# Denominators of a decayed linear attention: sums over weighted keys, or a scan of key states

## The reference, cut to what matters

```python
q = elu(x @ Wq) + 1 ; k = elu(x @ Wk) + 1 ; v = x @ Wv       # per head
a = sigmoid(x @ Wa + ba + 2)                                 # one decay per token and head
def step(carry, inp):
    S, z = carry
    qt, kt, vt, at = inp
    S = at * S + kt[:, None] * vt[None, :]
    z = at * z + kt
    num = einsum('k,kv->v', qt, S)
    den = einsum('k,k->', qt, z) + 1e-6
    return (S, z), num / den
out = scan(step) ; x1 = layernorm(x + out @ Wo)
```

## Time and profile before

| what | value |
|---|---|
| median of three runs | 1390.17 us |
| profiled execution, its own time | 1394.7 us |
| its span | 1392.8 us |
| linear attention stage | about 0 to 686 us of the span |
| PE busy in the steady part (360 to 420 us) | 59.19 of 60 us |
| DVE, ACT, POOL busy there | 36.08, 47.96, 26.02 of 60 us |
| granted clock of TensorE there | 1.00 |

### The profile page before, as it was taken

How to read it: one execution, slowest core, us unless ns; L and a number is a source line. 1 busy time by engine, 2 the same in 40 slices (tenths; PEclk the granted TensorE clock), 3 DMA queues, 4 the chain that set the end, 5 groups by cost and what they waited for, 6 DMA issues and landing times. The chain is left out here.

```text
span 1392.8 us, 29331 instructions
## 1 busy us (share of the span) xinstructions
PE 1255.3 (90%) x10053; PEld 1079.5 (78%) x10053; DVE 868.1 (62%) x1579; ACT 937.6 (67%) x2118; POOL 715.1 (51%) x645
## 2 busy tenths in 40 slices
PE   5999999999999999999899999944999999997870
PEld 4788888888888888887677777724788888887870
DVE  4456565665656565565468888845566666665664
ACT  3778777787777778787557777735465556655553
POOL 1244433444443344444467777701477777776653
PEclk9999999999999999999999999965899999999895
DMA  5232222322222232222134434323466666666638
GB/s 175 90 103 85 93 84 65 90 69 85 77 93 77 64 90 68 87 69 84 56 99 111 106 94 115 89 55 110 129 159 159 159 159 159 158 153 148 175 54 249
DMA packets 155787, 151.27 MB, mean 109 GB/s; under 512 B 48882, under 2 KB 124250, under 8 KB 155674
## 3 DMA queue, kind: packets, MB, share of 16 engines
q1 hardware_dynamic: 140698, 129.18, 30.3%
q0 software_dynamic: 14976, 20.62, 8.3%
HBM read 113.45 MB, written 33.84 MB: 106 GB/s over the span
## 5 line engine op out<-in xcount | busy, mean ns | idle before, releaser
L568 DVE SCALAR_TENSOR_TENSOR a_qk<-a_qk_exp,a_qk_relu 128x512 f32<-128x512 f32 x124 | 148.8, 1200 | 179.8 <-ACT a_qk_relu L416 179.8
L1889 POOL DMA_INDIRECT sum_rows<-e_y_out,e_target x78 | 128.0, 1642 | 81.9 <-ACT e_y_out L1943 58.3
L367 POOL TENSOR_TENSOR a_key_sum<-a_probs_old,a_probs_new 128x512 f32<-128x512 f32 x64 | 83.3, 1301 | 153.2 <-DVE a_probs_new L578 153.2
L360 POOL TENSOR_SCALAR_AFFINE_SELECT a_decay_old<-a_decay_old 128x512 f32<-128x512 f32 x64 | 40.6, 635 | 232.2 <-ACT a_decay_new L442 232.2
L676 PE MATMUL a_ps_qk<-a_xT_hi,a_w_hi 128*128 128x256 f32 x496 | 146.8, 296 | 6.8 <-ACT a_qk_relu L416 6.3
L676 PE MATMUL a_ps_qk<-a_xT_lo,a_w_hi 128*128 128x256 f32 x496 | 139.4, 281 | 0.0
L676 PE MATMUL a_ps_qk<-a_xT_hi,a_w_lo 128*128 128x256 f32 x496 | 139.3, 281 | 0.0
L440 ACT ACTIVATE a_decay_old<-a_c_rows,a_c_col 128x256 f32<-128x256 f32 x256 | 127.4, 498 | 17.6 <-DVE a_c_col L560 11.5
L415 ACT ACTIVATE a_qk_exp<-a_ps_qk 128x512 f32<-128x512 f32 x124 | 73.4, 592 | 95.8 <-PE a_ps_qk L676 95.3
L1870 POOL DMA_INDIRECT e_x_in<-x_rows,e_index x78 | 80.4, 1030 | 78.2 <-DVE e_index L2036 55.7
L576 DVE TENSOR_TENSOR a_probs_old<-a_ps_old,a_decay_old 128x512 f32<-128x512 f32 x128 | 82.3, 684 | 55.8 <-PE a_ps_o L768 44.3
(11 more groups left out here) (310 smaller groups left out, 4170.8 us busy)
## 6 DMA issues: line engine op xcount, KB each, us to landing
a_c_rows<-a_c_scratch SPq DMA_DIRECT2D x128, 256.0 KB, 3.4
e_gu_raw<-in_L_ffn_gate_w SPq DMA_DIRECT2D x23, 512.0 KB
e_gu_raw<-in_L_ffn_up_w SPq DMA_DIRECT2D x23, 512.0 KB
e_dn_raw<-in_L_ffn_down_w SPq DMA_DIRECT2D x23, 512.0 KB, 5.3
a_x_in<-in_x SPq DMA_DIRECT2D x16, 256.0 KB
a_resid<-in_x SPq DMA_DIRECT2D x16, 256.0 KB, 4.8
x_rows<-a_x SPq DMA_DIRECT2D x16, 256.0 KB, 3.4
x_bo_rows<-a_x_bo SPq DMA_DIRECT2D x16, 256.0 KB, 3.9
```

Source lines behind the costliest of these rows:

```text
L367: pool.tensor_tensor(key_sum[:], probs_old[:, :, P:N], probs_new[:], ALU.add).then_inc(keys_summed, 1)
L568: vec.scalar_tensor_tensor(qk[g][:], qk_exp[buffer][:], 1.0, qk_relu[buffer][:], ALU.min, ALU.add).then_inc(qk_done, 1)
L1889: pool.indirect_dma_start(sum_dram, bass.IndirectOffsetOnAxis(target[par][:, blk:blk + 1], 0), y_out[par][:, blk, :], None, compute_op=ALU ...
```

## The change

Denominators no longer come from the weighted scores. A scan on VectorE builds z for all 256 tokens: for a pair, `tensor_tensor_scan` of 128 features (two heads of 64) x 256 tokens with the decay a, spread over the features' partitions, and the keys. The states are multiplied by the queries on VectorE, split on GpSimd into fp32r parts (a cast and a subtraction), and summed over a head's 64 features by PE with a 128x128 tile that has two blocks of ones. `sum_states(b, k)` stands ahead of `weigh(b, k)` on VectorE, `split_sums` takes the place of `sum_keys` on GpSimd, and PE's `add_keys` of a batch is issued at the batch's end, behind the projections. ScalarE makes a once a sequence, and SyncE stores it and spreads it with four DMAs a batch, each to 64 partitions (L335 of the new kernel). The waits on `o_made` that guarded the weighted scores now are on `weighed`.

```diff
+            def spread_a(b, k):
+                m = b * BATCHES + k
...
+                if m >= 2:
+                    sp.wait_ge(states_done, 2 * (m - 1))
+                for h in range(2):
+                    for p in range(2):
+                        head = 4 * k + 2 * p + h
+                        sp.dma_start(a_rows[m % 2][h * DH:(h + 1) * DH, p, :],
+                                     a_dram[b, head:head + 1, :].to_broadcast([DH, N])).then_inc(a_loaded[m % 2], 16)
...
-            def sum_keys(b, k):
-
-                pool.wait_ge(probs_done, 3 * (b * BATCHES + k + 1))
+            def split_sums(b, g):
+                n = b * PAIRS + g
+                pool.wait_ge(q_states_done, n + 1)
+                if n >= 2:
+                    pool.wait_ge(o_made, n - 1)
                 pool.sem_inc(pool_turns, 1)
-                pool.tensor_tensor(key_sum[:], probs_old[:, :, P:N], probs_new[:], ALU.add).then_inc(keys_summed, 1)
+                pool.tensor_copy(sum_hi[g % 2][:], states[g % 2][:]).then_inc(sum_hi_done, 1)
+                pool.wait_ge(sum_hi_done, n + 1)
+                pool.tensor_tensor(sum_lo[g % 2][:], states[g % 2][:], sum_hi[g % 2][:].bitcast(F32), ALU.subtract)\
+                    .then_inc(sums_split, 1)
...
+            def sum_states(b, k):
+                m = b * BATCHES + k
+                vec.wait_ge(a_loaded[m % 2], 64 * (m // 2 + 1))
+                vec.wait_ge(qk_done, 2 * m + 2)
+                for p in range(2):
+                    if m:
+                        vec.wait_ge(sums_split, 2 * m - 1 + p)
+                    vec.tensor_tensor_scan(states[p][:], a_rows[m % 2][:, p, :], qk[2 * k + p][:, 1, :], 0.0,
+                                           ALU.mult, ALU.add).then_inc(states_done, 1)
+                for p in range(2):
+                    vec.wait_ge(states_done, 2 * m + 1 + p)
+                    vec.tensor_tensor(states[p][:], states[p][:], qk[2 * k + p][:, 0, :], ALU.mult).then_inc(q_states_done, 1)
 
             def weigh(b, k):
                 m = b * BATCHES + k
                 vec.wait_ge(s_made, 2 * m + 2)
-                vec.wait_ge(o_made, 2 * m)
+                vec.wait_ge(weighed, 2 * m)
...
                 for k in range(BATCHES):
+                    sum_states(b, k)
                     weigh(b, k)
...
-                for h in range(2):
-                    pe.matmul(out[h][:, 1, 0:P], ones[:], probs_old[:, 2 * h + p, 0:P], start=True, stop=True)
-                pe.wait_ge(keys_summed, m + 1)
-                for h in range(2):
-                    mm = pe.matmul(out[h][:, 1, P:N], ones[:], key_sum[:, 2 * h + p, :], start=True, stop=True)
-                mm.then_inc(o_made, 1)
...
+            def add_keys(b, g):
+                pe.wait_ge(sums_split, b * PAIRS + g + 1)
+                if b * PAIRS + g >= 2:
+                    pe.wait_ge(oT_done, b * PAIRS + g - 1)
+                pe.matmul(ps_o[g % 2][:, 1, :], head_ones[:], sum_hi[g % 2][:], start=True, stop=False,
+                          skip_group_check=True)
+                pe.matmul(ps_o[g % 2][:, 1, :], head_ones[:], sum_lo[g % 2][:], start=False, stop=True,
+                          skip_group_check=True).then_inc(o_made, 1)
...
                         if k in (1, 2):
                             project_v(b + 1, k - 1, 1)
+                    for p in range(2):
+                        add_keys(b, 2 * k + p)
```

More of the change, by code:

```diff
@@ L167, in sem @@
             return sh.semaphore(nc, name)
-        w_raw = [sb(f"a_w_raw{n}", [P, KC, PW]) for n in range(2)]
+        with nc.sbuf_tensor("a_w_raw0", [P, KC, PW], F32) as first_raw:
+            pass
+        states = [sb(f"a_states{n}", [P, N]) for n in range(2)]
+        sum_hi, sum_lo = ([sb(f"a_sum_{x}{n}", [P, N], F32R) for n in range(2)] for x in ("hi", "lo"))
+        a_rows = [sb("a_a_rows0", [P, 2, N])]
+        w_raw = [first_raw, sb("a_w_raw1", [P, KC, PW])]
         w_hi = [sb(f"a_w_hi{n}", [P, KC, PW], F32R) for n in range(3)]
@@ L178, in linear_attention @@
         ident = cross.ident
-        ones, scan_ones = sb("a_ones", [P, DH]), sb("a_scan_ones", [H, N])
+        head_ones, scan_ones = sb("a_head_ones", [P, P], F32R), sb("a_scan_ones", [H, N])
         x_in, resid = sb("a_x_in", [P, NB, D]), sb("a_resid", [P, NB, D])
@@ L228, in linear_attention @@
         decay_exp, decay_masked, probs_done = sem("a_decay_exp"), sem("a_decay_masked"), sem("a_probs_done")
-        keys_summed, o_made, ln_done, rden_done = (
-            sem("a_keys_summed"), sem("a_o_made"), sem("a_ln_done"), sem("a_rden_done"))
+        a_made, a_stored = sem("a_a_made"), sem("a_a_stored")
+        a_loaded = [sem(f"a_a_loaded{n}") for n in range(2)]
+        states_done, q_states_done = sem("a_states_done"), sem("a_q_states_done")
+        sum_hi_done, sums_split, weighed = sem("a_sum_hi_done"), sem("a_sums_split"), sem("a_weighed")
+        o_made, ln_done, rden_done = sem("a_o_made"), sem("a_ln_done"), sem("a_rden_done")
         oT_done, oT_hi_done, oT_lo_done, y_added = (
@@ L315, in sequence @@
                         store_c(b + 1)
+                        store_a(b + 1)
                     if ahead < B * PAIRS:
                         spread_c(ahead // PAIRS, ahead % PAIRS)
+                    for batch in range(b * BATCHES + g // 2 + 2, min(b * BATCHES + g // 2 + 3, B * BATCHES)):
+                        if g % 2 == 1:
+                            spread_a(batch // BATCHES, batch % BATCHES)
                     if g == 0 and b + 2 < B:
@@ L345, in _ @@
                                pattern=[[-1, P]], channel_multiplier=1).then_inc(ident_ready, 1)
-            pool.memset(ones[:], 1.0).then_inc(consts_step, 1)
+            pool.memset(head_ones[:].bitcast(F32), 0.0).then_inc(consts_step, 1)
+            pool.wait_ge(consts_step, 2)
+            for h in range(2):
+                rows = slice(h * DH, (h + 1) * DH)
+                pool.memset(head_ones[rows, rows].bitcast(F32), 1.0).then_inc(consts_step, 1)
+                pool.wait_ge(consts_step, 3 + h)
             pool.memset(scan_ones[:], 1.0).then_inc(consts_step, 1)
             pool.memset(eps_col[:], LN_EPS).then_inc(consts_step, 1)
-            pool.wait_ge(consts_step, 4)
+            pool.wait_ge(consts_step, 6)
             pool.memset(den_eps[:], EPS).then_inc(consts_ready, 1)
@@ L423, in log_decay @@
                 act.activation(decT[:], z_sb[:], ACT.Ln, bias=1.0).then_inc(dec_done, 1)
+                act.wait_ge(dec_done, b + 1)
+                act.activation(z_sb[:], decT[:], ACT.Exp, scale=-1.0).then_inc(a_made, 1)
             def keep_v(b, par, half, blk):
@@ L449, in invert_den @@
                 act.wait_ge(o_made, n + 1)
+                act.wait_ge(weighed, n + 1)
                 if n >= 2:
```

25 lines of the change are left out of this document (20 added, 5 removed).

## The result

The changed kernel takes 1424.44 us (median of 4 runs, 1423.78 to 1425.48) against 1391.15 us for the kernel before in the same session (4 runs, 1389.93 to 1392.67). The ratio is 1.0227, 95% interval 1.0206 to 1.0248: slower. The forecast was 1416 us, range 1386 to 1438. The profiled execution took 1425.48 us with a span of 1423.9, against 1394.7 and 1392.8 before.

A forecast was written before the change was run, and what follows sets the result against it. It took TensorE as the bound before and a ring through VectorE and ScalarE after: 14.75 sequences x (42.5 - 40.67) = +27, taken as +26 us, onto the 1390.2 median gives 1416 us, range 1386 to 1438.

The forecast's parts named there:

- the ring: Linear attention stage: `weigh`, decay Exps, Relu, `finish_qk`, next `weigh` in turn; 33.07 us a sequence before, 42.5 after.
- The holding: VectorE's first scan stands until GpSimd's second subtraction ends: 0.65 us in three of four batches, 1.95 a sequence.
- `weigh` to decays: Ring link from `weigh`'s start to the first decay Exp: 2.00 us in three batches, 3.27 in batch 3.
- The ring runs whatever PE does: Linear attention stage: the ring's steps follow each other independently of TensorE, whose own bound falls to 38.95 us a sequence.
- The ends, counted at nothing: Before the stretch and in the last sequence, VectorE's idle time covers the new instructions; the tail may shift 1 us.
- TensorE's idle time: Linear attention stage: TensorE's waits grow to some 3.5 us a sequence, most on `normalise` and the Relu.
- The forecast lengths by batch: Steady sequence after the change: batch 0 about 11.2 us, batches 1 and 2 10.6, batch 3 about 10.2.
- TensorE stays the bound: Rival, linear attention stage: TensorE sets the pace and the change gains 25 us, to 1365; chance 8%.
- Scans not held: Rival: GpSimd does not hold VectorE's scans; ring 40.5 us a sequence, time 1388 us; chance 12%.
- Held in part: Rival: Relu comes after both GpSimd subtractions in more batches; ring about 41.2, +8 us, to 1398; chance 14%.
- Held more: Rival: products wait for GpSimd's casts, `finish_qk` for a split subtraction; ring 43.9, +48 us, to 1438; chance 13%.
- Late decays: Rival: SyncE waits for scans before sending c rows; a microsecond a batch would be +59, to 1449; chance 3%.

The follow-up runs named there:

- Late scans: Changed kernel with `sum_states` of the next batch issued behind VectorE's other work, ahead of its wait for the Relu; 1374.75 us, ratio 0.9856 to the kernel before.
- the doubled products: Changed kernel with TensorE's new key products issued twice at the end of the batch; 1441.43 us, ratio 1.0337 to the kernel before.
- the run with one product: Changed kernel with one key product a pair, the product with the low part left out; 1418.49 us, ratio 1.0208 to the kernel before.
- the products one batch back: Changed kernel with TensorE's key products issued one batch later, behind that batch's late `weighted_values`; 1424.07 us, ratio 1.0217 to the kernel before.
- The run with two columns: Changed kernel with scans and products on 2 columns, not 256, except in the first batch; 1379.2 us, ratio 0.9891 to the kernel before.

## Why the prediction came out as it did

**What bounds before and after: right.** TensorE before, a ring through VectorE and ScalarE after, and the bound changes hands. (One reading on the way was wrong: the ring's slack of 7.6 us is not "the Relu wait of rows 2". That wait is 148.9 us from 100 to 650 us before, 11.0 a sequence, and with no slack left in the ring VectorE still waits for the Relu for 123.8 us, 9.5 a sequence. Nothing was computed from it.) Late scans (39.26 us a sequence against 42.43) show it by undoing only the place in VectorE's queue.

**The ring: right in sum, 42.30 against 42.46 (42.43 and 42.5 by the stretch), in part by luck, since two errors go opposite ways.** By the table, ScalarE's stretches and Relu to scan came within 0.04 and 0.02 us. Scans and products: 1.83 us a batch unheld against 1.86. The holding was mis-sized: 3 x 0.54 = 1.62 us of the sequence, not 1.95. The time for which the subtraction ran beside the scan was right (from 328.15 to 328.81, 0.66 us; 0.65 forecast), but the scans became longer by 0.53 only, so a held scan does not lose all of that time. The prediction's own rows had this: its held `finish_qk` at 20.21 lay 1.82 us beside the cast and took 2.37 where it takes 0.67 alone, a loss of 1.70, that is 0.12 less; and 0.66 less 0.12 is 0.54. Against it, `weigh` to decays was mis-sized the other way, 9.48 against 9.27: the forecast read its 2.00 us where nothing stood before the decays, and did not ask what ScalarE's queue holds ahead of them when TensorE's projection is late (0.17 us in batch 2); and in its 3.27 of batch 3 it took `finish_qk` at 0.60 to the next start, where it takes 0.66 beside GpSimd's splits.

**"The ring runs whatever PE does": wrong in batches 2 and 3.** It is the sentence that the doubled products broke (+1.06 us a sequence for 1.8). In this kernel it costs 0.17 us, as the run with one product shows, so the time was not hurt; but it is why every shortening of the ring gave less than its size (2.17 freed, 1.2 gained by the links; 5.04 freed, 2.9 gained). The prediction used a maximum of two bounds over a sequence. There are two bounds in each batch, and TensorE comes into batches 2 and 3 long before it would take the whole sequence.

**The ends, counted at nothing: wrong, +5.2 us, the largest part of the miss.** The first batch is a round of the ring like the others, and its 1.84 us are the 1.83 of an unheld `sum_states`; the 3.43 us of cover that the prediction named lie ahead of the first `weigh` (which came only 0.06 us later), not ahead of the second. In the last sequence, 1.48 of 2.70 us are in the batch that begins with a long wait of TensorE:

```profile
682.41 0.36 PE L836 MATMUL a_ps_o<-a_sum_hi,a_head_ones 128*128 128x256 f32 x1 [3.03 <-POOL a_sum_lo L411]
...
683.29 0.79 PE L800 MATMUL a_ps_old<-a_qk 64*128 64x256 f32 x1
...
691.04 0.48 PE L800 MATMUL a_ps_old<-a_qk 64*128 64x256 f32 x1
```

Without projections to do, TensorE reaches `add_keys` of batch 0 early and stands until GpSimd's split is over (682.35), with the scores of batch 1 queued behind. They then run at a lower clock, as the stretches of TensorE show (us, busy times with their counts, granted clock in the column before the last two):

```profile
676.00:682.00 6.00, 1.98 (x14) 1.54 (x12) 5.27 (x9) 2.26 (x6) 4.20 (x7) 1.00 0.26 71
682.00:687.00 5.00, 4.59 (x28) 3.64 (x30) 2.43 (x6) 3.47 (x10) 2.26 (x5) 0.66 0.58 177
687.00:692.00 5.00, 4.14 (x38) 3.44 (x35) 3.90 (x8) 3.73 (x10) 2.86 (x6) 1.00 0.20 66
```

After 6 us in which TensorE was busy for 1.98, the granted clock is 0.66 in the mean of the next five, a mixture of 2.4 and 1.2 GHz. With the products one batch back, `weigh` of batch 1 follows that of batch 0 by 6.40 us, as before (6.38), instead of 7.88, and the clock is 1.00 in the same stretches. By the rows nearly all of the loss is the clock's: from the first score's start to that of the weighted values it is 686.32 - 683.29 = 3.03 us, and 1.60 one batch later at full clock. Without those 1.43 us `weigh` would come at 686.5 (an estimate from these rows), where GpSimd's masks, over at 686.32, release it anyway. The other runs agree: the batch takes 7.75 to 8.30 us in all those with a stretch of low clock in it, and 6.38 to 6.93 in the four without. No run has the long wait without the low clock.

VectorE's idle time before that `weigh` (3.51 us, for TensorE) is nearly what it was (3.85); the cover was there, but the chain that ended last ran past it. The other 1.2 us are in batches 2 and 3 (0.5 and 0.7). In both, GpSimd's masks, on which `weigh` waits, take turns with VectorE's new instructions. VectorE and GpSimd in batch 2 of the last sequence:

```profile
692.20 1.26 DVE L628 TENSOR_TENSOR_SCAN a_states<-a_a_rows,a_qk 128x256 f32<-128x256 f32 x2
693.38 1.56 DVE L632 TENSOR_TENSOR a_states<-a_states,a_qk 128x256 f32<-128x256 f32 x2
694.87 1.28 DVE L640 TENSOR_TENSOR a_probs_old<-a_ps_old,a_decay_old 128x512 f32<-128x512 f32 x2
```

```profile
692.99 0.91 POOL L400 TENSOR_SCALAR_AFFINE_SELECT a_decay_old<-a_decay_old 128x512 f32<-128x512 f32 x1 [2.97 <-ACT a_decay_new L490]
693.85 0.82 POOL L400 TENSOR_SCALAR_AFFINE_SELECT a_decay_new<-a_decay_new 128x512 f32<-128x512 f32 x1
```

The masks take 0.91 and 0.82 us, not the 0.64 that each takes where VectorE is idle, and the products 1.56, not 0.73. The run with two columns bears on this. There both masks of batch 2 take 0.64, and the batch takes 6.40 us, as before, not 6.92: its 0.5 us are these columns. Batch 3 takes 7.28 there, against 6.69 before and 7.38 in the changed kernel, so most of its 0.7 us has another cause. Its `weigh` waits for TensorE:

```profile
657.25 1.29 DVE L640 TENSOR_TENSOR a_probs_old<-a_ps_old,a_decay_old 128x512 f32<-128x512 f32 x2 [2.50 <-PE a_ps_o L828]
```

In the changed kernel too it waits for TensorE last, 0.17 us at 702.24, and in both kernels TensorE has stood for GpSimd's split before it (0.65 and 0.64 us). How that batch's time divides between the two was not tested.

**TensorE's idle time: right in size, wrong in place.** 3.1 us a sequence against 3.5. The largest part is in batch 1, where the projection of v waits for `keep_v` on ScalarE (15.9 of 40.2 us), which the prediction did not name. `normalise` ahead of `add_keys` has 6.7. The forecast lengths by batch (11.2, 10.6, 10.6, 10.2) don't follow from the prediction's own links, which give 9.9, 10.4, 10.4 and 11.7 from `weigh` to `weigh`; measured there are 9.80, 10.43, 10.43 and 11.64.

**From 1416 to 1424.4.** The stretch is 0.1 below the forecast, the ends add 5.2. The last 3.2 belong to no cost in the working but to the step from the profile to the median: before's profiled execution lay 4.5 us above its median, after's only 1.0 above (+3.5; and own time and span differ by 1.6 where it was 1.9, -0.3). That is how single executions scatter, and chance for the forecast.

**The rivals.** TensorE stays the bound: it does with late scans, not here. Scans not held: no, 0.53 us in three batches of four. Held in part (41.2, one batch of four held): no, three are held, each for less than was thought. Held more, by products waiting for the new casts: not in the steady part (0.65 us for two, start to next start, throughout). Late decays: no wait for them in the views of waits.

## What to carry to other kernels

When work moves from the busiest engine to a slack one, look for a loop in which the slack engine's output comes back to it through single buffers; work added between "input came" and "output released" is paid in every round, and the same work issued behind the release, in the engine's wait, may be free. Here that choice was worth 3.6% (ratios 1.0227 and 0.9856). Compute the bound per stage of the period and not only over all of it, and count the first and last periods as rounds, since there another engine's work no longer hides a wait.
